# Attention with the weighing matmuls of two steps issued together

## The reference

```python
attn = jnp.einsum('bqd,bkd->bqk', q, k) / np.sqrt(HD)
rel_bias_h = jnp.einsum('bhwc,hkc->bhwk', rq, Rh)
rel_bias_w = jnp.einsum('bhwc,wkc->bhwk', rq, Rw)
attn = (attn.reshape(b * NH, h, w, h, w) + rel_bias_h[:, :, :, :, None] + rel_bias_w[:, :, :, None, :]).reshape(b * NH, hw, hw)
attn = jax.nn.softmax(attn, axis=-1)
out = jnp.einsum('bqk,bkd->bqd', attn, v)
```

## Time and profile before

| | |
|---|---|
| median of three runs | 967.38 us (964.85 to 968.34) |
| the profiled execution | 966.49 us, its span 964.5 us |
| attention in the span | from about 232 to 835 us |
| PE busy | 837.1 us, 87% |
| DVE busy | 742.2 us, 77% |
| ACT busy | 559.6 us, 58% |
| POOL busy | 410.9 us, 43% |
| mean granted clock of TensorE | 0.918 |

### The profile page before, as it was taken

The page is one execution under the profiler, slowest core; times in us unless marked ns, Lnnn a source line. Parts: engine busy times, 40 slices in busy tenths (PEclk is TensorE's granted clock), DMA queues, the critical chain, the costliest instruction groups (busy, mean ns, idle before and its releaser), DMA issues. The chain is left out here.

```text
span 964.5 us, 15322 instructions
## 1 busy us (share of the span) xinstructions
PE 837.1 (87%) x5848; PEld 424.7 (44%) x5848; DVE 742.2 (77%) x1512; ACT 559.6 (58%) x654; POOL 410.9 (43%) x223
## 2 busy tenths in 40 slices
PE   5799479558999999999999999999999999678875
PEld 2465356223444444444444444444444443256643
DVE  7666465169888888888888888888888885179993
ACT  1332333012677777777777777777777778457663
POOL 1445602032637364544445363736363333123442
PEclk9899755557999999999999999999999999889886
DMA  6576449979974939292929293958668000332411
GB/s 148 169 234 203 173 145 218 245 220 198 194 122 107 174 88 191 68 196 68 203 60 200 54 212 69 193 89 169 112 147 135 12 13 12 124 116 98 131 34 49
DMA packets 65674, 130.05 MB, mean 135 GB/s; under 512 B 9465, under 2 KB 45306, under 8 KB 57146
## 3 DMA queue, kind: packets, MB, share of 16 engines
q1 hardware_dynamic: 65602, 129.08, 58.2%
HBM read 89.73 MB, written 34.60 MB: 129 GB/s over the span
## 5 line engine op out<-in xcount | busy, mean ns | idle before, releaser
L1040 DVE TENSOR_REDUCE at_piece_neg<-at_r_ps 128x1 f32<-128x512 f32 x768 | 483.6, 681 | 71.2 <-PE at_r_ps L908 71.2
L1004 ACT ACTIVATE at_probs<-at_s_ps 128x1024 f32<-128x1024 f32 x384 | 372.0, 1021 | 155.1 <-PE at_s_ps L932 155.0
L908 PE MATMUL at_r_ps<-op_mix_k,op_mix_q 128*128 128x256 f16 (+1 forms) x1920 | 282.9, 257 | 24.1 <-DVE at_piece_neg L1040 20.2
L908 PEld LDWEIGHTS at_r_ps<-op_mix_k,op_mix_q 128*128 128x128 f16 x1920 | 149.6, 99 | 290.4 <-DVE at_piece_neg L1040 203.6
L828 POOL COPY op_mix_q<-op_mix_q 2x4096 f16<-2x4096 f16 x48 | 172.6, 3596 | 235.0 <-ACT op_mix_q L1010 234.5
L932 PE MATMUL at_s_ps<-op_mix_q,op_mix_k 128*128 128x512 f16 x768 | 227.6, 379 | 1.1 <-ACT at_probs L1004 0.6
L946 PE MATMUL at_o_ps<-at_probs,op_v_u 128*32 128x512 f32 x1536 | 204.1, 604 | 0.0
L218 POOL MEMSET op_mix_q<- 2x10240 f32 x12 | 103.5, 8627 | 25.9 <-DVE op_v_u L1181 25.3
L932 PEld LDWEIGHTS at_s_ps<-op_mix_q,op_mix_k 128*128 128x128 f16 x768 | 73.6, 98 | 19.1 <-ACT at_probs L1004 10.4
L690 DVE TENSOR_TENSOR op_mix_q<-rb_b_ps,op_mix_q 128x512 f16<-128x512 f32 (+1 forms) x36 | 29.5, 863 | 58.5 <-ACT op_mix_q L677 58.5
L1010 ACT ACTIVATE op_mix_q<-at_r_ps 2x512 f16<-2x512 f32 x96 | 51.7, 583 | 38.8 <-PE at_r_ps L921 38.3
(11 more groups left out here) (119 smaller groups left out, 665.8 us busy)
## 6 DMA issues: line engine op xcount, KB each, us to landing
op_mix_q<-qk_parts SPq DMA_DIRECT2D x48, 640.0 KB, 11.4
op_mix_q<-bias_parts SPq DMA_DIRECT2D x120, 120.0 KB, 10.6
bias_parts<-op_mix_q SPq DMA_DIRECT2D x12, 1024.0 KB, 7.2
op_mix_q<-bias_parts SPq DMA_DIRECT2D x72, 128.0 KB, 10.2
qk_parts<-op_mix_q SPq DMA_DIRECT2D x24, 256.0 KB, 2.4
v_rows<-pr_v_st SPq DMA_DIRECT2D x8, 768.0 KB, 4.4
op_mix_k<-qk_parts SPq DMA_DIRECT2D x48, 128.0 KB, 13.3
op_v_u<-v_rows SPq DMA_DIRECT2D x12, 512.0 KB, 14.3
```

The lines of the kernel that those rows point to most:

```text
L908: last = pe.matmul(r_bank("piece", at)[:, first % GROUP:first % GROUP + n], mix_q[owner.buf][:, variant, j, qt * P:(qt + 1) * P], mix_k[ow ...
L1004: act.activation(probs[n % PRING][:, 2 * pair:2 * pair + 2, :], s_ps[pair][:, :, :], ACT.Exp).then_inc(exp_done, 1)
L1040: dve.tensor_reduce(piece_neg[half][:, i:i + 1], r_bank("piece", at)[:, :], AX_X, ALU.max, negate=True).then_inc(reduced, 1)
```

## The change

The weighing of a step is no longer issued in every step. In an even step none is issued; in an odd step n the weighings of steps n - 3 and n - 2 are issued one directly behind the other, at the place where one stood. A weighing of an even step so comes one step later than before, that of an odd step where it was. Every engine executes the same instructions as before. The first step pair of the first unit has nothing to weigh. After the last unit's last step the weighings of its last two steps follow as before.

```diff
--- before.py
+++ after.py
@@ -982,10 +982,11 @@
                         scores(unit, n, j)
                     for at in todo[BEFORE[QUAD]:AFTER]:
                         piece(unit, at)
-                    if n >= LAG:
-                        weigh(unit, n - LAG)
-                    elif not unit.first:
-                        weigh(unit.after(-1), STEPS + n - LAG)
+                    for at in (n - LAG - 1, n - LAG) if n % 2 else ():
+                        if at >= 0:
+                            weigh(unit, at)
+                        elif not unit.first:
+                            weigh(unit.after(-1), STEPS + at)
                     for at in todo[AFTER:]:
                         piece(unit, at)
```

## The result

The changed kernel takes 988.54 us (987.23 to 989.83, four runs) against 967.82 us before: the ratio is 1.022, 95% interval 1.0195 to 1.0246. It is slower by 20.7 us; the forecast was 985, +17 to +18. The profiled execution has a span of 988.0 us against 964.5 before, 23.5 us more; it is the longest of the four.

What follows compares the result with a forecast made beforehand. TensorE, VectorE and ScalarE were taken as close, with double weighings exposing waits for VectorE's banks and ScalarE's exponentials. Halves 13.4 plus last unit 4.7 gave +18.1 us: 984.6 profiled, 985.5 against the median, forecast 985, range 975 to 991.

Steps and rivals of the forecast that it cites:

- What a double weighing costs: On TensorE, two adjacent weighings take 1.86 us (1.00 + 0.86); with one entry of 0.10 saved, 0.24 less per pair.
- Plain pair: Two steps without turn or inversion: TensorE waits for a PSUM bank VectorE must free, 5.85 us against 5.68, +0.17.
- ScalarE's chain: In a plain pair, exponentials between one double weighing and the next: 5.74 us, against TensorE's own work of 5.45.
- Pair with the inversion: Two steps where VectorE also inverts the sums (0.90 us in the bank chain): 6.75 against 6.10, +0.65, the largest term.
- Turn pairs: Pairs with the transposed maxima, which take two of three banks: 6.68 us against 6.68 and 6.85, 0.00 and -0.17.
- Half a unit: Eight steps of attention, four pairs, 25.31 us before: +0.65 us each, over 22 halves +14.3 us.
- trim of 0.01 per pair: Deduction for rounded links taken to come out a little long: 0.9 us in all, 14.3 to 13.4 us.
- Last unit: End of attention, no pieces from step 5 on: double weighings leave ScalarE without scores, pairs 5.09 against 4.25; +4.7 us.
- The output copy: At steps 1 and 9, waits about 0.9 us longer for the pair's second weighing; covered by more than a microsecond, less maxima's copies.
- Start of attention: No term of its own; the very first pair, which has nothing to weigh, was left uncounted.
- Hidden at nothing: Waits counted as zero: probability buffer reuse, output copy, and POOL's clearing and SP's loads, waiting for step 1's weighing as before.
- The first rival: TensorE stays the bound and saved switches are everything: 944 us, if VectorE's and ScalarE's chains are shorter than forecast; 8%.

Runs made afterwards that it cites:

- e5: Changed kernel with VectorE reducing 128 of a piece's 512 columns and ScalarE taking exponentials of 128 of a head's 512 queries: 926.2 us, ratio 0.9568.
- e6: Kernel before (one weighing a step) with reductions over 128 of 512 columns and exponentials of 128 of 512 queries: 941.9 us, ratio 0.9731.
- e3: Changed kernel with VectorE's inversion of the sums, its spread and GpSimd's scaling cut to 32 of 512 queries: 973.9 us, one run.
- e9_late_pieces_two: Changed kernel with score pieces later in each step, scores of heads 0 and 1 first: 977.3 us, ratio 1.0111.

## Why the prediction was right, and where it was off

Sign and mechanism were right; the predicted 985 stands 3.5 us under the 988.5. The sum was made for the profiled executions, and these differ by 23.5 us, not 18.1: 2.8 us of the difference lie in the halves, 2.8 in the start of attention, and the last unit gives 0.1 back. That the median came closer than the profile is no merit of the sum.

- *What a double weighing costs* (1.86, 0.24 saved per pair): 1.86 in the trace of the changed kernel, and 0.24 where nothing waits (e5 against e6).
- *Plain pair* 5.85 by the banks: 5.86. *ScalarE's chain* 5.74 as the second bound: 5.75 once the reductions are short.
- *Pair with the inversion* 6.75: 6.74, and 6.82 in every second half. The 0.08 belong to the half with the unit's fifth step, where TensorE's program also waits for the next unit's loads and clearing; the prediction had that only in its range. The kernel before has the 0.08 too (6.10, the half that was read, against 6.02), but there the turn pair behind took it up (6.84 against 6.92). So this pair became 0.72 dearer in both halves, not 0.65. In the pair that was looked at, the loads had landed 17 us before TensorE asked for them (548.27 against 565.27 us), so what costs the 0.08 is open.
- *Turn pairs* 6.68: 6.71 both. The chain runs over ScalarE, as its four exponentials without a gap from 531.29 show. Link by link it is 2.10 to the first exponential (529.19 to 531.29; 2.08 forecast), 1.94, 0.06 to the next scores (0.05 forecast), 0.75 and 1.86.
- *Half a unit* +0.65 less a trim of 0.04: +0.71 and +0.78. This is the mis-sized term: 21 measured halves give 15.6 us, where the forecast of 13.4 for 22 gives 12.8 for 21. The trim of 0.01 per pair went the wrong way; the untrimmed 14.3 gives 13.7. One link checked against one row is no ground for a correction.
- *Last unit* +4.7: +4.6, four pairs of 5.09 as forecast to the digit. The turn pair came out at 5.91 instead of 6.13, the one before at 5.61 instead of 5.53.
- *The output copy*, hidden at nothing: it stayed hidden, by less than the microsecond forecast. Behind it and the maxima's copies ScalarE is still idle for 0.28 us before its exponentials (the row at 531.29).
- *Start of attention*: +3.4 in the profiled execution, where the forecast had the 0.6 of one half. The step "Hidden at nothing" listed SP's loads as waiting for the same weighing as before, which is so; it missed the other direction, TensorE waiting for a load. In the trace of before this wait is 0.65 us long, and a weighing moved from in front of a wait to behind it is paid in full, 0.86. The rest of the start is not the change's alone: 0.46 is a load that landed later, and 1.63 a clock that fell in this execution and not in e3's, which waited longer.

The first rival had its saving right and its condition wrong: a bank chain 0.17 us shorter would only bring a plain pair back to 5.68, no change. For the saving both chains must come down to TensorE's 5.45, by 0.40 and 0.29, as e5 made them.

The Trainium skill's rule (TensorEngine Tiling, Key Properties: a change of tiling mode drains the engine) agrees with the light kernels, which show 0.24 us for one way in and out; it did not decide.

## What to carry to other kernels

Merging two stalls of a producer into one is worth the overhead saved only while its consumers' buffers outlast the merged stall: here three banks of 0.60 us against 1.00 us alone or 1.86 together. Work out the cycle through each consumer, including the second one, since removing one bound uncovers the next. Where a producer has a long instruction group that the full buffers outlast, try filling them right in front of it first: for a group of 1.00 us against three banks of 1.8, moving one piece by one place won as much as the grouping lost. For the group of 1.86 us, which they don't outlast, the same move won nothing.

## What the runs showed of the hardware that was not expected

- The way out of the weighing depends on what follows. Before a piece (full array) the distance from a weighing's start is 1.00 us, before the turn, whose matmuls also go to a 32-column strip, it is 0.90 (495.99 to 496.89 above).
- An idle stretch of 2.19 us of TensorE was followed by a granted clock of 0.62 over 4.5 us, in the first unit of the changed kernel, and one of 2.04 us at the same place in e9_late_pieces_two by a granted clock of 0.66 from 250 to 255 us. But e3_small_inverse_two was idle for 2.36 us there and kept 1.00, as did the kernel before with 0.65. In the last unit of the changed kernel, where 1.05 us are idle in every 5.09, it stayed at 1.00. So the length of one idle stretch doesn't settle it.
